# Backward projections without their bias product; VectorE evacuates them and adds the bias

## The reference

```python
def _typed_pass(feat, W, bias, src_idx, dst_idx, etypes, norm_per_edge, n):
    proj = jnp.einsum('ni,rio->rno', feat, W)
    m = proj[etypes, src_idx] + bias
    m = m * norm_per_edge[:, None]
    return segment_sum(m, dst_idx, num_segments=n)
...
m_forward = _typed_pass(feat, Wf, forward_bias, src, dst, etypes, norm_f, n)
m_backward = _typed_pass(feat, Wb, backward_bias, dst, src, etypes, norm_b, n)
s = feat @ loop_weight
s = s + s + self_bias
return s + m_forward + m_backward
```

## Time and profile before

| what | value |
|---|---|
| median of 3 runs | 3746.93 us |
| profiled execution | 3745.95 us |
| its span | 3744.1 us |
| PE busy | 3223.3 us (86%) |
| weight loads (PEld) busy | 2773.1 us (74%) |
| DVE busy | 2459.1 us (66%) |
| ACT busy | 1001.8 us (27%) |
| POOL busy | 2492.3 us (67%) |
| chain that ended last | PE 43%, POOL 26%, issue 13%, DVE 12% |

### The profile page before, as it was taken

The page is one execution under the profiler, slowest core; times in us unless marked ns, Lnnn a source line. Parts: engine busy times, 40 slices in busy tenths (PEclk is TensorE's granted clock), DMA queues, the critical chain, the costliest instruction groups (busy, mean ns, idle before and its releaser), DMA issues.

```text
span 3744.1 us, 73443 instructions
## 1 busy us (share of the span) xinstructions
PE 3223.3 (86%) x21136; PEld 2773.1 (74%) x21137; DVE 2459.1 (66%) x3369; ACT 1001.8 (27%) x1563; POOL 2492.3 (67%) x3139
## 2 busy tenths in 40 slices
PE   5999999999999996999877788877867787877776
PEld 4999999999999995788666666666656666665654
DVE  6899999999999998887666663232254444444333
ACT  3555555555555554443111111111120000000000
POOL 1777777777777770001777777777777777777775
PEclk8999999999999998999999999999989999999999
DMA  5666666656656662565555557555543333333333
GB/s 165 174 174 178 173 177 172 176 168 178 172 171 173 170 171 74 195 209 191 162 167 165 162 167 175 168 162 160 165 116 105 105 105 105 105 105 105 105 105 114
DMA packets 322756, 570.00 MB, mean 152 GB/s; under 512 B 73896, under 2 KB 218392, under 8 KB 322584
## 3 DMA queue, kind: packets, MB, share of 16 engines
q0 software_dynamic: 137984, 411.19, 39.2%
q1 hardware_dynamic: 182732, 154.33, 12.9%
q10 hardware_dynamic: 1868, 2.52, 0.2%
HBM read 452.43 MB, written 115.41 MB: 152 GB/s over the span
## 4 chain that ended last, share of the span: by engine, by line
PE 43%; POOL 26%; issue 13%; DVE 12%; DVEq 1%; DMA 1%; ACT 1%; POOLq 0%; ACTq 0%
POOL hr L431 18%; PE pc L681 14%; PE pa L691 10%; PE pu L671 5%; DVE tops L1242 4%; PE pg L655 4%; DVE key L1245 4%; POOL fa L431 4%; PE pu L663 3%; POOL ws L431 2%; PE pc L643 1%; POOL rows_b L431 1%; PE pu L787 1%; POOL rows_a L431 1%; DVE onehot L1014 1%
## 5 line engine op out<-in xcount | busy, mean ns | idle before, releaser
L412 POOL DMA_INDIRECT fa<-ptab,slot x784 | 774.8, 988 | 325.9 <-issue 254.9
L431 POOL DMA_INDIRECT hr<-proj,row_dst x784 | 741.4, 946 | 238.7 <-issue 238.4
L431 POOL DMA_INDIRECT fa<-proj,row_src x400 | 379.7, 949 | 466.6 <-DMA proj<-fa 343.5
L681 PE MATMUL pc<-ws,hr 128*128 128x256 f32 x4704 | 603.9, 284 | 0.0
L681 PEld LDWEIGHTS pc<-ws,hr 128*128 128x128 f32 x4704 | 570.9, 189 | 0.7 <-issue 0.7
L1014 DVE SCALAR_TENSOR_TENSOR fa<-pc,base,src_f 128x1024 f32<-128x1024 f32 (+1 forms) x210 | 260.6, 1248 | 137.8 <-issue 131.2
L691 PE MATMUL pa<-fa,onehot 128*128 128x256 f32 x904 | 240.0, 416 | 113.9 <-DVE onehot L1014 52.6
L733 PE MATMUL pu<-hr,fa 128*128 128x258 f32 x1056 | 248.4, 388 | 89.3 <-issue 50.3
L691 PEld LDWEIGHTS pa<-fa,onehot 128*128 128x128 f32 x904 | 179.5, 205 | 169.3 <-issue 138.7
L733 PE MATMUL pg<-hr,fa 128*128 128x258 f32 x1040 | 242.1, 385 | 70.9 <-issue 54.2
L733 PE MATMUL pa<-hr,fa 128*128 128x258 f32 x1040 | 241.7, 384 | 68.4 <-issue 46.8
(11 more groups left out here) (167 smaller groups left out, 5748.3 us busy)
## 6 DMA issues: line engine op xcount, KB each, us to landing
proj<-fa SPq DMA_DIRECT2D x400, 256.0 KB, 2.3
fa<-in_ea_t SPq DMA_DIRECT2D x196, 128.0 KB, 3.3
fa<-ptab,slot POOLq DMA_INDIRECT x784
hr<-proj,row_dst POOLq DMA_INDIRECT x784, 2.7
fa<-in_Wrel SPq DMA_DIRECT2D x32, 256.0 KB, 3.2
ptab<-fa SPq DMA_DIRECT2D x25, 256.0 KB, 2.0
fa<-proj,row_src POOLq DMA_INDIRECT x400, 3.0
ws<-proj,row_src POOLq DMA_INDIRECT x192, 3.0
```

What stands on the lines that cost most here:

```text
L412: pool.indirect_dma_start(pbuf[:, n % 2, j, :], None, ptab[:, :], bass.IndirectOffsetOnAxis(ap=slot[:, n, j:j + 1], axis=0)).then_inc(s_ga ...
L431: pool.indirect_dma_start(buffer[:, j, 0:H], None, table, bass.IndirectOffsetOnAxis(ap=rows[:, J * s + j:J * s + j + 1], axis=0)).then_inc ...
L681: last = nc.tensor.matmul(pc[:, j, :], uT[:, par, a, j // 2, kk, j % 2 * P:(j % 2 + 1) * P], w2s[:, c, kk, :], start=False, stop=(j == jj ...
```

## The change

The backward projections lose their bias matmul. The bias is loaded once as a row copied over all 128 partitions (`bbias_b`). VectorE evacuates a backward block from PSUM with the bias added; ScalarE no longer touches the backward blocks, and keeps only the high half of each weight split. VectorE does block m at the end of iteration m, after it has added supertile s-1 and made the further one-hot of s; at the end of a pair (m = 23) it does blocks 23 and 24.

```diff
-        bias_k = sb("bias_k", [P, 2, H], F32R)
+        bias_k = sb("bias_k", [P, 1, H], F32R)
+        bbias_b = sb("bbias_b", [P, H])
...
-            for d, bias in enumerate((b2, bbias)):
-                act.dma_start(bias_raw[:, d, :], bias.to_broadcast([2, H])).then_inc(s_w, 16)
+            act.dma_start(bias_raw[:, 0, :], b2.to_broadcast([2, H])).then_inc(s_w, 16)
+            act.dma_start(bbias_b[:, :], bbias.to_broadcast([P, H])).then_inc(s_w, 16)
...
             with act.Fori(NQ // 4, NQ // 2 - 1) as i:
-                relations(i, True)
-            relations(NQ // 2 - 1, False)
+                for u in range(2):
+                    weights_high(2 * i + u + 1, 1 - u, i + u)
+            weights_high(NQ - 1, 1, NQ // 2 - 1)
...
-            def project(q, u, b, d):
+            def project(q, u, b):
 
                 n = b % 5
                 if b >= 5 or past(q, 1):
                     pe.wait_ge(s_pev[n], 5 * q + b // 5)
-                if d:
-                    nc.tensor.matmul(pslots[n].rearrange("p (r f) -> p r f", r=2), ones_k[:, :],
-                                     bias_k[:, 1:2, :].to_broadcast([P, 2, H]), start=True, stop=False)
...
-            split_row(bias_k[0:2, :, :], bias_raw)
+            split_row(bias_k[0:2, 0:1, :], bias_raw)
...
+            def evacuate_backward(q, b):
+
+                n = b % 5
+                dve.wait_ge(s_proj, NB * q + b + 1)
+                dve.wait_ge(s_pst[n], 16 * (5 * q + b // 5))
+                nc.vector.tensor_tensor(pstage[n], pslots[n].rearrange("p (r f) -> p r f", r=2),
+                                        bbias_b[:, :].unsqueeze(1).to_broadcast([P, 2, H]), ALU.add).then_inc(s_pev[n], 1)
+
...
                         next_block(s, w[m % GS + 1])
+                        evacuate_backward(q, m)
+                        if m == QS - 1:
+                            evacuate_backward(q, NB - 1)
```

More of the change, by code:

```diff
@@ L121, in gnn_program @@
         wtop = fa[:, 9216:10240].rearrange("p (k f) -> p k f", k=HK)
-        bias_raw = fa[0:2, 6144:6144 + 2 * H].rearrange("p (d f) -> p d f", d=2)
+        bias_raw = fa[0:2, 6144:6144 + H].rearrange("p (d f) -> p d f", d=1)
         bias_raw2 = fa[DE:DE + 2, 6144:6144 + H].rearrange("p (d f) -> p d f", d=1)
@@ L787, in project @@
                         last = nc.tensor.matmul(pslots[n], hT[:, a, kk, b * P:(b + 1) * P], wsp[:, u, c, kk, :],
-                                                start=(not d and m == 0 and kk == 0), stop=(m == 2 and kk == HK - 1))
+                                                start=(m == kk == 0), stop=(m == 2 and kk == HK - 1))
                 last.then_inc(s_proj, 1)
@@ L794, in forward_relations @@
                     for b in range(NB):
-                        project(2 * i + u, u, b, 0)
+                        project(2 * i + u, u, b)
             for g in range(NB // GB):
@@ L803, in _ @@
                     pe.wait_ge(s_hT[1], b + 1)
-                    project(0, 0, b, 0)
+                    project(0, 0, b)
             pe.wait_ge(s_wlo, 2)
             for b in range(NB):
-                project(1, 1, b, 0)
+                project(1, 1, b)
             with pe.Fori(1, NQ // 4) as i:
@@ L821, in _ @@
                     for b in range(AHEAD):
-                        project(q, u, b, 1)
+                        project(q, u, b)
                     for m in range(QS):
                         if m + AHEAD < NB:
-                            project(q, u, m + AHEAD, 1)
+                            project(q, u, m + AHEAD)
                         t = QS * u + m
@@ L903, in _ @@
             nc.vector.memset(res[:, NB - 1, :], 0.0).then_inc(s_xzero, 1)
-            nc.vector.memset(bias_k[:, :, :].bitcast(F32), 0.0)
+            nc.vector.memset(bias_k[:, 0, :].bitcast(F32), 0.0)
             link(nc.vector.memset(ones_k[:, :].bitcast(F32), 1.0))
```

## The result

Over five runs of each kernel in turn on one chip, the changed kernel takes 3765.74 us (median; 3761.97 to 3772.01), the kernel before 3745.11 us (3741.78 to 3748.16). The ratio is 1.0058, with a 95% interval of 1.0046 to 1.0069: 0.6% slower, where "no change that can be measured" was the likeliest case. It lies at the upper edge of the whole range (3747 to 3766) and outside of the forecast's own (3748 to 3755). The profiled execution took 3765.59 us, its span is 3763.8 us against 3744.1.

A forecast was written before the change was run, and what follows sets the result against it. GpSimd's gathers, one each 1.25 us, were taken as the bound. Profiled 3745.95 us + 0 (TensorE) + 0 (VectorE) + 4.3 (turn) = 3750.3, as a median 3751.2 us; own range 3748 to 3755, whole range 3747 to 3766.

The forecast's parts named there:

- no change that can be measured: Case of a time within 0.2% (7.5 us) of the kernel before; given a chance of 0.64.
- the turn: From last forward to first backward gather, GpSimd waits for the last stored backward projection: 4.3 us later.
- TensorE's relief pays: Rival: the chain through TensorE is the bound, so its 46 us less work shows, about 3705 us; chance 0.03.
- The second gather: The gather after the first backward one: possibly 1.9 us more from an empty queue, kept only in the range.
- The wait behind the sorted keys: In iteration 5, ScalarE's 13.87 us wait for a store becomes VectorE's, 6 to 8 us, covered.
- 0 (VectorE's work, covered by the slack): Term of the sum: 200 added evacuations on VectorE delay sums in the forward gather stage without stalling GpSimd; 0 us.
- lateness of 12.8 us at supertile 100: Delay of the consumer's addition at supertile 100: 18.5 us added less 5.7 us given back.
- the evacuations: VectorE's added work in the sorting cycles: 0.4 to 0.45 us a cycle, 44 x 0.42 = 18.5 us.
- slack of 16.7: Time from the 101st forward addition to the 429th gather, which needs supertile 100's sum; forecast read 16.8 us.
- The relief of TensorE: 200 fewer bias matmuls: 46 us less work, 0 at the end; turns between pairs and the first group give back 5.7 us.
- VectorE drains the slack: Rival: evacuations cost 0.77 us a cycle, GpSimd stalls 11.4 us before supertile 100's sum, 3762.6 us; chance 0.27.
- The room that I forecast: Slack left at supertile 100 after the consumer's delay: 16.8 - 12.8 leaves 4 us, no stall.

The follow-up runs named there:

- e2_scalar: The kernel before without the bias matmul of the backward projections, bias left out, ScalarE still evacuating: 3745.8 us, ratio 1.0003 to the kernel before.
- e1_kept: The changed kernel with one thrown-away matmul of the bias's size ahead of each backward projection: 3763.7 us, ratio 1.0047 to the kernel before.
- e5_three: The changed kernel with three thrown-away matmuls of the bias's size ahead of each backward projection: 3749.7 us, ratio 1.0013 to the kernel before.
- e8_scalar_three: The kernel before with two thrown-away matmuls ahead of each backward bias matmul, ScalarE still evacuating: 3745.0 us, ratio 1.0001 to the kernel before.
- e3_odd: The changed kernel with blocks m - 1 and m both evacuated in the odd m, behind the one-hot: 3751.6 us, ratio 1.0012 to the kernel before.
- e9_in_wait: The changed kernel with two evacuations between one-hot and addition of each even m, the last three blocks at m = 22: 3746.7 us.
- e10_even: The changed kernel with blocks m and m + 1 both evacuated in the even m, between addition and next sort: 3809.6 us.
- e4_early: The changed kernel with each pair's last two backward blocks evacuated at m = 22, behind block 22: 3769.5 us, ratio 1.0067 to the kernel before.

## Why the prediction was wrong

**The frame was right.** GpSimd's 1.25 us a gather bound the kernel, the relief of TensorE gained nothing at the end (e2_scalar: 1.0003), and what counted were a stall and the turn. The rival that TensorE's relief pays went by the shares of the whole span, where TensorE's weight loads lead (74% against 67%). In the forward gather stage alone GpSimd leads them, 744.52 against 633.04 of 985 us (PE, PEld, DVE, ACT, POOL busy, clock, DMA share, GB/s, before the change):

```profile
1755.00:2740.00 985.00, 791.10 (x3290) 633.04 (x3290) 470.86 (x784) 124.56 (x207) 744.52 (x785) 0.95 0.57 164
```

That would have spoken against this rival as the cadence does.

**The turn was right.** VectorE's evacuation takes 0.69 us, as taken. I gave the turn 4.3 us; it went from 2.55 to 6.17, so 3.6, and GpSimd's wait ended with a DMA of `proj`. The second gather after it wasn't late (1.27 us), so the 1.9 us that I kept in the range are nothing here. The wait behind the sorted keys is VectorE's now and costs nothing, as said, though it is 9.88 us and not 6 to 8:

```profile
2333.43 0.69 DVE L1311 TENSOR_TENSOR fa<-pu,bbias_b 128x512 f32<-128x512 f32 x1 [9.88 <-DMA proj<-fa]
```

**The step that failed** is the term "0 (VectorE's work, covered by the slack)". It stood on a lateness of 12.8 us at supertile 100: 44 x 0.42 = 18.5 us for the evacuations, less 5.7 us that the missing bias matmuls give back. Measured were 34.8 us against a slack of 16.7. Both parts were mis-sized, by 9.5 and 12.5 us, which together are the 22.0 us between forecast and measurement:

- *The evacuations.* I gave them 18.5 us; with TensorE's work unchanged (e1_kept against before) they cost 28.0. The row that I read was right: the sort is pushed back by 0.49 us (1.36 in place of 0.87), where I had 0.42. Where the clock stays high (e5_three against e8_scalar_three) the move costs only 11.8 us, less than my 18.5. What I left out is that VectorE's longer cycle lowers TensorE's clock itself, from 0.94 to 0.90, and makes the sums longer. (That 11.8 and the 12.8 of the forecast are close is luck: the 12.8 hold the 5.7 us given back, and those two kernels have nothing to give back.)
- *The relief of TensorE.* I booked it as -5.7 us of lateness and as 0 in the sum. At the four turns from pair to pair (28th to 29th addition, and each 24 further) e2_scalar does win back 1.8, 2.2 and 1.7 us, and nothing at the fourth (-0.2), against my 1.2 each. Over the whole stretch it is 10.5 us later all the same, and the changed kernel is 6.8 us later than e1_kept. I asked only whether less work on TensorE can make the end earlier; the granted clock falls with it, and the sums that VectorE waits for become longer.

With both, TensorE's waits for one-hots from 1800 to 2300 us grow, and the time at the lower clock with them. Before, e2_scalar and the changed kernel:

```profile
PE pa L691 <- DVE onehot L1014: 76.2, 40, 5.0
```

```profile
PE pa L691 <- DVE onehot L1011: 108.2, 41, 7.8
```

```profile
PE pa L693 <- DVE onehot L1013: 118.3, 41, 7.3
```

The stall needs the low clock and the place of the evacuation together: raising the clock (e5_three) and moving the evacuation at the same low clock (e3_odd) each take 20.9 us of lateness away. Why slow sums cost so little in e3_odd and so much in the changed kernel, where as many are slow, stays open beyond that; the 9.5 and 12.5 us come from single executions. GpSimd's stall, 1001.7 - 982.6 = 19.1 us, is what 34.8 us of lateness leave over the slack of 16.7, within 1.0 us. Stall and turn make 22.7 us; the forward gathers started 2.7 us earlier, which leaves 20.0; the span grew by 19.7.

**The rival was the case.** "VectorE drains the slack" has the right place, the right buffer and the right waits, and its 3762.6 us is near. That is in part luck. Its price was put down to the whole of an evacuation in each cycle (0.77 us), which isn't what happened: with the rival's own 5.7 us taken back, (34.8 + 5.7) / 44 is 0.92 us a cycle, of which the sort that is pushed back is 0.49, and the rest came with the lower clock. I named the clock there in half a sentence and gave it no price, though the earlier trace rows show 0.93 and the earlier trace rows a matmul at either level. The room that I forecast was 4 us: three slow sums more, at 1.8 us each, would use it up, and there were 19 more.

The Trainium skill (Perfetto Trace Analysis, Optimizing Scalar/DVE Operations) says that where VectorE is saturated, moving some of its work to ScalarE may make sense. e9_in_wait and e10_even have the same 200 evacuations on VectorE, and 63 us lie between them: what decided was the place in the chain, not VectorE's share. The Trainium skill (TensorE: Matmul & The Clock Gate, Loop structure matters more than you think) marks a copy out of PSUM by VectorE as one that leaves TensorE's clock up, for a loop whose matmuls stand back to back. At three matmuls the clock is 0.96 with ScalarE and 0.97 with VectorE, which agrees. With one it is 0.94 and 0.90; this isn't that loop, for TensorE waits there for one-hots that VectorE makes between its copies.

## What to carry to other kernels

Work taken from TensorE isn't always free where TensorE waits in a chain with another engine: read the granted clock of that stretch, count the products that run at either level, and price more of them before you write a zero. Where the slack is shared, add up all terms that draw on it, those of a relief too: here the relief alone was free, the move alone cost 0.5% (e1_kept), both together 0.6%. And price added work on an engine of such a chain at the clock that it leaves behind, not at the clock of the trace before. Put the work of an evacuation into the wait that its engine has, between the issue of the operand and the use of the product, not in front of the next link of the chain.

## What the runs showed of the hardware

- Matmuls that nobody needs can save time: three of them ahead of each backward projection (0.23 us each) took the changed kernel from 3765.7 to 3749.7 us with the clock of the stretch at 0.97 in place of 0.86. Against the kernel before they gain nothing.
- A sum of eight matmuls takes 1.99 us at 2.4 GHz and 3.78 at 1.2; the level changed from cycle to cycle, 28 falls in 500 us in the changed kernel and 13 before.
- The same 200 matmuls less (0.94 to 0.88) and 200 evacuations more on VectorE (0.94 to 0.90, TensorE's work unchanged) both lowered TensorE's granted clock from 1800 to 2300 us.
- A store of 256 KB near the end of the forward gathers landed after 2.2 to 5.4 us. Three in a row took 5.1 to 5.4 us (e4_early), 2.4 to 3.6 (e9_in_wait) or 2.3 to 2.5 (e3_odd, behind the last gather), so their number doesn't decide.
